# Column-order projection: memory-order reads with a stepped PSUM write, and diagonal copies in smaller groups

## The reference, cut to what matters

```python
x_flat = xa.reshape(B, D_INNER, L)                      # L = 64 * 64, D_INNER = 192
x_wh = xa.transpose(0, 1, 3, 2).reshape(B, D_INNER, L)  # columns first
x_hwwh = jnp.stack([x_flat, x_wh], axis=1)
xs = jnp.concatenate([x_hwwh, jnp.flip(x_hwwh, -1)], axis=1)   # K = 4 directions
x_dbl = jnp.einsum('bkdl,kcd->bkcl', xs, x_proj_w)      # 6 + 16 + 16 = 38 rows
...
delta = jax.nn.softplus(dts + dt_proj_b[None, :, :, None])
...
dA = jnp.exp(dl[..., None] * A)
h = dA * h + (dl * ul)[..., None] * Bl[:, :, None, :]
y = jnp.einsum('bkdn,bkn->bkd', h, Cl)
```

## Time and profile before

| | |
|---|---|
| median of 3 runs | 12486.86 us |
| profiled execution, its own time | 12466.46 us |
| its span | 12464.6 us |
| busy PE / DVE / ACT / POOL | 10542.2 / 10742.0 / 8078.1 / 9756.1 us |

### The profile page before, as it was taken

One profiled execution on the slowest core, in us unless ns is written; L12 is line 12 of the kernel. 1 busy time (PEld: TensorE's weight loads), 2 busy tenths in 40 slices (PEclk: granted clock), 3 DMA queues, 4 the chain that ended last, 5 costly groups with the idle time before them and its releaser, 6 DMA issues. The chain is left out here.

```text
span 12464.6 us, 232157 instructions
## 1 busy us (share of the span) xinstructions
PE 10542.2 (85%) x89848; PEld 5478.0 (44%) x89848; DVE 10742.0 (86%) x6806; ACT 8078.1 (65%) x13314; POOL 9756.1 (78%) x4238
## 2 busy tenths in 40 slices
PE   8978888888888888888888888888888887799999
PEld 5633333333333333333333333333333333678778
DVE  7789999999999999999999999999999998555554
ACT  3366777776777677777776777677777775444443
POOL 2188989999999899989998999899999998433330
PEclk9978888888888888888888888888888887899999
DMA  3344554455545554554455545544554454221220
GB/s 107 111 110 112 122 132 114 112 126 131 116 114 125 128 117 115 125 130 115 113 126 128 117 115 126 129 116 114 124 130 112 115 122 113 71 61 47 62 62 11
DMA packets 380176, 1363.43 MB, mean 109 GB/s; under 512 B 55271, under 2 KB 55975, under 8 KB 375757
## 3 DMA queue, kind: packets, MB, share of 16 engines
q1 hardware_dynamic: 379084, 1348.57, 45.9%
HBM read 983.45 MB, written 364.90 MB: 108 GB/s over the span
## 5 line engine op out<-in xcount | busy, mean ns | idle before, releaser
L939 POOL TENSOR_TENSOR HC<-H,crep 128x1024 f32<-128x1024 f32 x3072 | 7197.6, 2368 | 523.0 <-DVE H L756 388.8
L756 DVE TENSOR_TENSOR_SCAN H<-E,car,psum 128x1024 f32<-128x1024 f32 x1920 | 4483.0, 2344 | 279.3 <-PE psum L650 148.2
L609 PE MATMUL psum<-sx,selb 96*128 96x512 f32 x4864 | 2074.0, 523 | 1495.4 <-DVE H L756 1330.8
L840 ACT ACTIVATE E<-dlr,am 128x1024 f32<-128x1024 f32 x2560 | 2912.7, 1144 | 47.6 <-DVE H L756 43.7
L672 PE MATMUL psum<-HC,sely 128*32 128x512 f32 x12288 | 2640.9, 726 | 34.2 <-POOL HC L939 34.2
L609 PEld LDWEIGHTS psum<-sx,selb 96*128 96x128 f32 x4864 | 913.9, 229 | 3306.6 <-DVE H L756 2045.8
L734 DVE TENSOR_TENSOR psum<-dur,psum 128x1024 f32<-128x1024 f32 x1792 | 2168.1, 1210 | 152.5 <-PE psum L609 149.1
L650 PE MATMUL psum<-diag,dluT 128*32 128x128 f32 x49152 | 1902.7, 309 | 157.4 <-DVE H L756 142.8
L650 PEld LDWEIGHTS psum<-diag,dluT 128*32 128x32 f32 x49152 | 1587.7, 125 | 830.1 <-DVE H L756 587.9
L756 DVE TENSOR_TENSOR_SCAN H<-E,psum 128x1024 f32<-128x1024 f32 x640 | 1458.7, 2285 | 87.0 <-PE psum L650 35.0
L824 ACT ACTIVATE diag<-idn,blt 128x128 f32<-128x128 f32 x4096 | 1278.8, 389 | 70.1 <-PE psum L650 66.1
(11 more groups left out here) (135 smaller groups left out, 10708.1 us busy)
## 6 DMA issues: line engine op xcount, KB each, us to landing
dur<-scr_dlu SPq DMA_DIRECT2D x1024, 384.0 KB, 6.9
dlr<-scr_dl SPq DMA_DIRECT2D x1024, 384.0 KB, 6.7
scr_dl<-dlt SPq DMA_DIRECT2D x256, 384.0 KB, 3.0
scr_dlu<-dlu SPq DMA_DIRECT2D x256, 384.0 KB, 8.6
scr_yk<-yt SPq DMA_DIRECT2D x256, 384.0 KB, 6.6
yp<-scr_yk SPq DMA_DIRECT2D x128, 384.0 KB, 9.0
scr_xa<-xs SPq DMA_DIRECT2D x64, 384.0 KB, 3.5
scr_sz<-xs SPq DMA_DIRECT2D x64, 384.0 KB, 3.4
```

The source lines that it names most:

```text
L609: r = e.matmul(o[:, sub * 512:(sub + 1) * 512], selb[:, which, :], sx[:, c % 2, sub * 512:(sub + 1) * 512], start=True, stop=True)
L756: e.tensor_tensor_scan(H[:, un % NH, ::step], decay[:, ::step], drive[:, ::step], init, ALU.mult, ALU.add).then_inc(scan_done)
L840: e.activation(o, dlr[:, slot(m, j), :], ACT.Exp, scale=am[:, ae:ae + 1]).then_inc(exp_done)
L939: e.tensor_tensor(HC[:, un % NHC, :], H[:, un % NH, :], crep[:, g, :], ALU.mult).then_inc(hc_done)
```

## The change

In column directions `project` no longer reads `u` in column order. It reads the 64 rows one after the other, in each the 8 neighbouring columns of its block, and puts the results where they belong by a stepped write: from one element to the next the PSUM address goes up by 64 floats, and after 8 of them the next row starts one float further. The values in `stage` are the same, at the same places. Row directions are as before. And ACT's 16 diagonal copies at x = 6 are split: 8 stay, and 8 come at x = 7 behind `turn_dlu`.

```diff
@@ -589,9 +589,14 @@
+            o = stage[0:C + NR, sub * 512:(sub + 1) * 512]
+            if k % 2:
+                o = o.rearrange("p (w h) -> p h w", h=HW)
             for h in range(2):
-                r = e.matmul(stage[0:C + NR, sub * 512:(sub + 1) * 512], wx[:, k, h, :], view(k, h, t0, 512),
-                             start=h == 0, stop=h == 1)
+                x = u[:, h, t0:t0 + 512]
+                if k % 2:
+                    x = u[:, h, :].rearrange("p (h w) -> p h w", w=HW)[:, :, t0 // HW:(t0 + 512) // HW]
+                r = e.matmul(o, wx[:, k, h, :], x, start=h == 0, stop=h == 1)
             if sub:
                 r.then_inc(x_done)
 
@@ -901,9 +906,10 @@
                     rep(c, 0)
                     diagonal(c, 0, 3)
                 if x == 6 and c < NCHUNK:
-                    diagonal(c, 3, 16)
+                    diagonal(c, 3, 8)
                 if x == 7 and c < NCHUNK:
                     turn_dlu(2 * c)
+                    diagonal(c, 11, 8)
                 if x == 8 and c < NCHUNK:
                     diagonal(c, 19, 3)
```

## The result

The changed kernel takes 12263.83 us (median of 4 runs, 12261.45 to 12268.64), the kernel before beside it 12484.67 us; the ratio is 0.9821, 95% interval 0.9804 to 0.9838. Later runs gave 12254.14 us and a ratio of 0.9823 (0.981 to 0.9837).

What follows compares the result with a forecast made beforehand. DVE was taken to bound the kernel, its idle time being the possible gain. 48 x 2.42 + 16 x 2.93 = 163 us, with the copies at 0, took 12486.86 to 12324 us; whole range 12275 to 12505 us.

Steps and rivals of the forecast that it cites:

- What bounds the kernel: Scan phase: DVE sets the pace, and the gain available is its idle time, about 621 us over 128 chunks.
- The read at 0.43 us a pass: Column projection's operand read in runs of 8 floats: costs 0.43 us a pass, as a plain row does.
- The write at 0.43 us: Column projection's stepped PSUM write: costs 0.43 us a pass, taken with less trust than the read.
- rival 3: Column projection: stepped write slower than the old stepped read, at 1.71 us a pass about 12890 us; chance 0.13.
- Rivals 1, 2 and 3: Projection's stepped write at 0.86 us a pass (12487 us, 0.17); at 0.6 (12389 us, 0.08); at 1.71 (12890 us, 0.13).
- What 3.42 us less on PE is worth: DVE's gain in 64 chunks holding a column projection: 2.42 us in 48, 2.93 us in 16, together 163 us.
- The lower end of the range: Whole kernel: fastest time in the whole range, 12275 us; all of PE's saving would give 12268.
- The in-between rival: Column projection: a pass at 0.6 us, saving 2.1 of 3.42 us, so 98 us, 12389 us; chance 0.08.
- The copies: ACT's split diagonal copies: cost between 0 and 22 us through a softplus 0.7 us later; taken as 0.
- Rival 4: ACT's new copy order hurts in every chunk, 90 us, 12577 us if the write gives nothing too; chance 0.02.

Runs made afterwards that it cites:

- e3: The changed kernel with the projection's operand read in runs of 2 floats instead of 8, the write stepped accordingly; 12268.72 us.
- e6: The changed kernel with three groups of twelve 2-byte matmuls (plain, stepped result, stepped operand) put before each projection, their results overwritten; 13556.36 us.
- e4: The changed kernel with the old read for the projections of chunks 7 and 15, made inside chunks 6 and 14; 12327.35 us.
- e11: The changed kernel with each column projection made twice in the new way into the same place; 12382.9 us, ratio to before 0.993.
- e5: The changed kernel with one half of the channels read the old way in column directions; 12289.76 us, ratio to before 0.9861.
- e2: The kernel before with only the diagonal copies split into two groups of eight; 12468.99 us beside 12469.25, ratio 0.9997.
- e7: The changed kernel, unaltered, run again on the same chip as the projection-only kernel; 12254.14 us.
- e8: The changed kernel with the sixteen diagonal copies in one group, second run, on the same chip as the changed kernel; 12246.84 us.
- e1: The changed kernel with the sixteen diagonal copies put back in one group, so only the projection is new, first run; 12254.08 us.
- e10: The changed kernel with three quarters of each column projection read the old way; 12454.98 us, ratio to before 0.9987.

## Why the prediction was right or wrong

**What bounds the kernel**: right. DVE's busy time in the page moved by 4 us, and the rest of the 202 us came out of its idle time.

**The read at 0.43 us a pass**: right, and e3 shows that runs of 2 would do. **The write at 0.43 us**: right for these passes, by e6 with nothing to spare. My reason was near but not sufficient, and there was some luck in it: DVE's reads showed only that 80 more elements cost 81 ns, stepped or not, 1.0 ns each, and the pass wanted one in 0.84; in e6 a stepped write took 0.83. The rule of the Trainium skill ("PSUM — Partial Sum Buffer", Specifications), by which I gave rival 3, agrees with e6 at the pace of 2-byte matmuls, where a step doubled the pass, and does not agree with the 4-byte passes, which took 3.60 us with the step and without. Rivals 1, 2 and 3 fell with that.

**What 3.42 us less on PE is worth**: this is the step that failed, in one term of the sum. I took 2.42 us for each of the 48 chunks that work in a column direction themselves, with chunk 7 as their model; they gained 3.02 each, 145.0 us against 116. Chunk 7 was no clean model: e4 shows that the extra idle time in it was left behind by the projection in chunk 6, and went with it. The 16 others gained 3.38 us each, not 2.93, in part because chunk 7 was also among the 56 from which the 2.93 came. Without it those are 48 chunks in (4229.60 - 611.30) / 48 = 75.38 us, and 64 x (78.46 - 75.38) would have been 197 us; all 64 gained 199.0, 3.11 each, where the sum had 163. That is 36 us of the error. The 56 other chunks gave 10.4 us that I had at nothing: 5.4 in the eight chunks 7 (611.30 to 605.90), for the reason that e4 shows, and 5.0 spread over the other 48, 0.1 each, for no reason that a run shows. The last chunks of the images took 6.6 back, which is within what they vary by (633.90 to 644.20 in four profiles with the new projection and no other read). The rest is in the comparison: I carried the 20 us between the profiled execution and the median over to the changed kernel, but there the profiled execution's 12262.3 us of span stands beside a median of 12263.83. So the profiled execution of before, 12466.46 us, was quicker than the four runs beside which the ratio was taken (12478.91 to 12501.84), and only 3 to 7 us below the medians since (12469.25 to 12473.19). 163 + 36 + 10 - 7 = 202 in the profiles, and 19 between them and the medians.

**The lower end of the range** was too high. I had written the bound itself, PE's whole saving of 219 us or 12268 us, and then set 12275; and with the scatter of the runs 12268 was no floor either. Nor, as an argument, was PE's saving a ceiling for DVE's gain: the fall of the clock outlasts the projection, so that its removal also speeds up what follows. I had read the 0.64 in the earlier trace rows and used it only to say that it was not the cause of the 7.02 us. That is true, but by e11 it goes with 1.21 us a chunk behind them.

**The in-between rival** was priced along a straight line, 98 us for 2.1 us saved. By e5, half of the old lateness costs 0.46 us a chunk and not 1.55. It didn't enter the forecast.

**The copies**: costed at 0 to 22 us, taken at 0. On the old projection they cost nothing (e2), on the new one about 7 us (e7 against e8) and perhaps up to 15 (e1 against e3). The range was right. My mechanism's first half, ACT idle before the transposes, is in the profile (104.1 us against 10.0); its second, a later softplus, is not seen, so where the cost arises stays open. Rival 4 is out.

## What to carry to other kernels

When an operand must be transposed on the way through a matmul, put the step where the pass has time to spare: in 4-byte matmuls a step in the result cost nothing and an operand without neighbours doubled the pass. Where a stage is to stand as a model for another, see first whether its own idle time was left there by a neighbour; a window over one chunk doesn't say whose fault its idle time is. And a slow stretch on PE is to be priced together with the clock behind it: here 1.21 of 3.11 us lay after the slow instructions had ended, in work that the change doesn't touch. The clock is then to be read in the changed kernel too, over whole chunks: it can be lost again in another place.

## What the runs showed of the hardware that I had not expected

- PE counted as busy through the whole stepped read, and the granted clock fell from 1.00 in the midst of it (0.64 in its second part, 0.52 in the next 4 us). In e11 it stayed at 1.00 through a projection of the same 7.0 us that streams at full pace. So PE, counted as busy throughout, lost its clock under the stepped reads and kept it under as long a run of passes at 0.43 us. It also kept it in e5's 5.30 us, where pairs of stepped and of new passes take turns.
- One 2-byte column takes 0.42 ns at 2.4 GHz, and 0.83 with a step of 64 floats in PSUM. With a step of 64 elements in the operand it takes 1.70, and a 4-byte one as long (0.86 us / 512 = 1.68), whether the granted clock is at 2.4 or at 1.2 GHz.
- In e10 two passes with the cheap read took the 0.86 us of the dear one, because the clock had been lost before them: with the last quarter of the projection mended, the kernel gained 15 of some 216 us.
- Removing the stepped reads did not raise the mean granted clock: 0.849 before, 0.842 after. The changed kernel has a stretch of 20.00 us at 0.50 where the kernel before had a mean of 0.74, and where it comes from is open.
